# Batch 1's quantised rows transposed by DMA from SyncE's queue in place of TensorE

## The reference

```python
q1 = fake_quant(layernorm(x), x1_scale, x1_zp)      # clip(round(v / s + z), 0, 255), then (q - z) * s
q2 = fake_quant(ctx_4096, x2_scale, x2_zp)
x = x + matmul(q1, q2)                              # per batch: [1024 x 2048] @ [2048 x 2048]
y = layernorm(x)
h = einsum('td,erd->ter', y, lora_A)                # 8 experts of rank 16, two chosen by a router
x = x + y @ W_base.T + b_base + einsum('ter,eor,te->to', h, lora_B, w) * 2.0
```

## Time and profile before

| | |
|---|---|
| median of 3 runs | 991.64 us |
| profiled execution, its own time | 990.91 us |
| its span, first to last instruction | 989.2 us |
| TensorE, matmul busy | 958.8 us (97%) |
| VectorE busy | 794.6 us (80%) |
| ScalarE busy | 429.1 us (43%) |
| GpSimd busy | 146.8 us (15%) |
| TensorE's granted clock | full in every slice |
| bytes moved by DMA | 185.66 MB, 188 GB/s on average |

### The profile page before, as it was taken

How to read it: one execution, slowest core, us unless ns; L and a number is a source line. 1 busy time by engine, 2 the same in 40 slices (tenths; PEclk the granted TensorE clock), 3 DMA queues, 4 the chain that set the end, 5 groups by cost and what they waited for, 6 DMA issues and landing times.

```text
span 989.2 us, 15078 instructions
## 1 busy us (share of the span) xinstructions
PE 958.8 (97%) x5829; PEld 525.3 (53%) x5829; DVE 794.6 (80%) x1471; ACT 429.1 (43%) x466; POOL 146.8 (15%) x184
## 2 busy tenths in 40 slices
PE   2999999999999999999999999999999999999998
PEld 1766666666699444444444444444444444444444
DVE  7998988989717887997875887757889788798786
ACT  4878887755533435554443552213232323322310
POOL 3645444455100000000000000000000000000000
PEclk9999999999999999999999999999999999999999
DMA  9967676877443337867665664168533143242220
GB/s 373 371 228 297 265 275 268 295 303 267 151 139 133 108 102 227 269 213 231 228 229 171 202 232 103 57 220 287 176 109 129 69 144 118 80 151 92 87 75 33
DMA packets 62312, 185.66 MB, mean 188 GB/s; under 512 B 6896, under 2 KB 19488, under 8 KB 56096
## 3 DMA queue, kind: packets, MB, share of 16 engines
q1 hardware_dynamic: 58648, 174.18, 49.5%
q0 software_dynamic: 1280, 2.12, 2.1%
q10 hardware_dynamic: 2312, 8.39, 2.1%
HBM read 151.07 MB, written 33.60 MB: 187 GB/s over the span
## 4 chain that ended last, share of the span: by engine, by line
PE 86%; DVE 0%; issue 0%
PE pair L1877 34%; PE pair L1901 29%; PE pair L1714 13%; PE pair L1839 5%; PE pair L1849 4%; PE pair L1913 1%; PE pair L1722 0%; PE pair L1819 0%; PE pair L1693 0%; PE pair L1734 0%; DVE sq L1563 0%; DVE xt L1018 0%; DVE u L1565 0%; PE pair L1728 0%; PE pair L1813 0%; PE pair L1738 0%
## 5 line engine op out<-in xcount | busy, mean ns | idle before, releaser
L1877 PE MATMUL pair<-x2p,w_p 128*128 128x512 f16 x1536 | 337.0, 379 | 0.0
L1877 PEld LDWEIGHTS pair<-x2p,w_p 128*128 128x128 f16 x1536 | 150.3, 98 | 180.4
L1714 PE MATMUL pair<-q1T,ctx_q 128*128 128x342 f16 (+2 forms) x1584 | 228.6, 305 | 4.8 <-DVE xt L1018 2.8
L1714 PEld LDWEIGHTS pair<-q1T,ctx_q 128*128 128x128 f16 x1584 | 152.7, 97 | 75.1 <-issue 3.8
L1901 PE MATMUL pair<-x2p,w_slot 128*128 128x512 f16 x744 | 163.8, 379 | 0.0
L836 ACT ACTIVATE sq<-pair,lsc 128x512 f32<-128x512 f32 x64 | 43.5, 681 | 210.2 <-PE pair L1849 174.3
L1638 POOL TENSOR_SCALAR ctx_u<-ctx_f,par 128x512 uint8<-128x512 f32 x128 | 114.2, 905 | 109.5 <-DMA ctx_f<-in_ctx 88.4
L1901 PEld LDWEIGHTS pair<-x2p,w_slot 128*128 128x128 f16 x744 | 72.7, 98 | 87.9
L864 ACT ACTIVATE w_slot<-w_q,usc 128x1024 f16<-128x1024 f32 x32 | 36.5, 1146 | 90.8 <-DVE usc L1469 27.2
L1901 PE MATMUL pair<-x2p,x2p 128*128 128x512 f16 x336 | 74.3, 379 | 0.0
L734 ACT ACTIVATE xt<-xt,colt 128x1024 f32<-128x1024 f32 x32 | 36.7, 1146 | 55.1 <-DVE xt L1018 55.1
(11 more groups left out here) (223 smaller groups left out, 1112.8 us busy)
## 6 DMA issues: line engine op xcount, KB each, us to landing
ctx_f<-in_ctx SPq DMA_DIRECT2D x32, 1024.0 KB, 7.4
xt<-in_xT SPq DMA_DIRECT2D x32, 512.0 KB, 4.6
w_r<-in_w_n SPq DMA_DIRECT2D x32, 512.0 KB, 7.3
w_f<-in_w_t SPq DMA_DIRECT2D x32, 512.0 KB, 5.9
w_q<-in_w_t SPq DMA_DIRECT2D x32, 512.0 KB, 4.9
outT<-u SPq DMA_DIRECT2D x63, 256.0 KB, 2.7
rows<-in_x SPq DMA_DIRECT2D x15, 1024.0 KB, 9.8
x_kept<-xt ACTq DMA_DIRECT2D x16, 512.0 KB, 4.3
```

The costliest lines, as they stand in the source:

```text
L1714: ins = M.matmul(bank[at % RING][:, 0:w], ctx_q[n % NQ][:, k, :], q1T[b][:, k, t0:t0 + w], start=(k == 0), stop=(k == KT - 1))
L1877: M.matmul(base_bank(m)[:, :], w_p[j % 2][wh][:, k, :], x2p[0][:, k, xh, t], start=(k == 0 and q == 0), stop=(k == KT - 1 and q == 2))
```

## The change

For batch 1 the eight `turn` calls of TensorE are gone, 64 transposes. SyncE issues one DMA transpose per tile in their place, from the bytes of the tile (seen as 128 x 1024 16-bit pairs) into a new buffer `q1t` in SBUF (two slots). It stands behind `load_ctx` and ahead of `load_rows`, and waits for the bytes and for the copy of the tile two before. ScalarE's `ln_copy` waits for the DMA's semaphore and reads `q1t` instead of the PSUM bank; `ln_bytes_of` waits for the transfer of the tile two before. `q1t` overlaps `ar_f`, whose load moves from step 15 to step 18 and waits for all copies. `stat_sums(0)` on TensorE moves behind two chunks.

```diff
+        q1t = [place(f"q1t{s}", [P, PAIRS, P], U16, ROW_AT[1] + 2 * D * 4 + 2 * D + s * D) for s in range(2)]
...
+        q1_moved = [sem(f"q1_moved{s}") for s in range(2)]
...
+            def turn_rows(T):
+                wait_bytes(sp, T)
+                if T - TT >= 2:
+                    sp.wait_ge(q1T_copied, T - 1)
+                sp.dma_start_transpose(q1t[T % 2][:, :, :], q1u[1][T % 2][:, :].bitcast(U16)).then_inc(q1_moved[T % 2], 16)
+
...
             load_ctx(4)
             load_ctx(5)
+            turn_rows(TT)
             load_rows(TT + 2)
             for n in range(3, STEPS):
                 load_xt(n)
                 if n + 3 < STEPS:
                     load_ctx(n + 3)
+                if n == 3:
+                    turn_rows(TT + 1)
+                if n - 3 in BYTES_AT:
+                    turn_rows(BYTES_AT[n - 3])
                 if n in LOAD_AT:
                     load_rows(LOAD_AT[n])
-                if n == JT - 1:
+                if n == JT + 2:
+                    sp.wait_ge(q1T_copied, ROWS)
                     sp.dma_start(ar_f[:, :, :], ar).then_inc(ar_landed, 16)
...
-                if T % TT >= 2:
+                if b and T - TT >= 2:
+                    act.wait_ge(q1_moved[T % 2], 16 * ((T - TT) // 2))
+                elif T % TT >= 2:
                     act.wait_ge(q1_turned, T - 1)
...
-                act.wait_ge(q1_turned, T + 1)
+                if b:
+                    act.wait_ge(q1_moved[T % 2], 16 * (t // 2 + 1))
+                    turned = q1t[T % 2][:, :, :].rearrange("p m t -> p (m t)")
+                else:
+                    act.wait_ge(q1_turned, T + 1)
+                    turned = turned_bank(T)
...
-                    stat_sums(0)
                     chunk(n - 1, 2)
                     chunk(n, 2)
+                    stat_sums(0)
                     continue
                 chunk(n, 0)
-                if n == 3:
-                    turn(TT)
-                if n == 4:
-                    turn(TT + 1)
                 chunk(n, 1)
...
                 chunk(n, 2)
-                if n - 2 in BYTES_AT:
-                    T = BYTES_AT[n - 2]
-                    turn(T)
```

More of the change, by code:

```diff
@@ L7 @@
 I32 = mybir.dt.int32
+U16 = mybir.dt.uint16
 U8 = mybir.dt.uint8
@@ L717, in ln_copy @@
                 b, t = T // TT, T % TT
-                act.wait_ge(q1_turned, T + 1)
+                if b:
[4 more added lines that the diff above has]
+                    turned = turned_bank(T)
                 A.activation(q1T[b][:, :, t * P:(t + 1) * P].rearrange("p (m e) t -> p m e t", e=2),
-                             turned_bank(T).bitcast(U8).rearrange("p (m t e) -> p m e t", m=PAIRS, e=2),
+                             turned.bitcast(U8).rearrange("p (m t e) -> p m e t", m=PAIRS, e=2),
                              ACT.Identity, bias=LO1).then_inc(q1T_copied, 1)
@@ L1645, in row_bytes_of @@
                 pool.wait_ge(ln_scale, g + 1)
-                if T % TT >= 2:
+                if b == 0 and T >= 2:
                     pool.wait_ge(q1_turned, T - 1)
@@ L1686, in turn @@
                 wait_bytes(pe, T)
-                if T >= TT:
-                    pe.wait_ge(q1T_copied, T)
-                elif T >= 2:
+                if T >= 2:
                     pe.wait_ge(q1T_copied, T - 1)
```

## The result

The changed kernel takes 1003.51 us, median of 4 runs (1002.75 to 1004.29). The kernel before takes 991.64 (median of 4, 991.61 to 991.66). The ratio is 1.012, interval 1.0102 to 1.0137. So the change is **11.9 us slower**. The forecast was 997.0, 5.4 slower, in a range up to 1010: the sign and the range hold, and the measured loss is 2.2 times the forecast's. The profiled execution is the slowest of the four: 1004.29 us, its span 1002.5 against 989.2, 13.3 more.

A forecast was written before the change was run, and what follows sets the result against it. VectorE's takes were taken to set TensorE's pace up to 139 us. Late copies and rows, 2.9 + 1.1 + 1.1 + 1.0 = 6.1, less 0.9 for turns, add 5.2 us: 996.1 profiled, median 997, range 988 to 1010.

The forecast's parts named there:

- the turns are worth nothing: TensorE, batch 1: six turns before 139 us worth nothing, those of T = 14 and 15 worth 0.9 us.
- the transfer lands 0.7 us behind the context: SyncE's queue, served in order: the tile's 256 KB at 370 GB/s take 0.7 us more after the context lands.
- SyncE's own issue I take at 0.4 us, as every other one: SyncE: issuing a transpose holds it 0.4 us, making the row load behind it 1.1 us later.
- a hold of over 1 us: Sign against the forecast: SyncE held for over 1 us by a transpose.
- the late rows: Row loads behind transposes: VectorE loses 1.0 us at T = 10, 1.1 each at T = 14 and 15.
- the late copies: ScalarE's copies waiting for landings: 2.9 us in full for T = 10, 0 for the other tiles priced.
- The room of 2.5 us for T = 14: After 139 us: the take of (14,1) ends 2.5 us before (15,2) needs it, absorbing lateness.
- none later: Sign: TensorE's idle time for takes grows before (13,2) by 6 us plus the turns' 2.6, and not after.
- The forecast had 6.1 there: Before 139 us: late copies and late rows, 2.9 + 1.1 + 1.1 + 1.0 = 6.1 us.
- Hidden: Rival 1: the transfer doesn't queue behind the context and costs nothing, 990.7 us; chance 0.28, within 2 us.
- TensorE gets its 3.5 us: Rival 2: VectorE's chain keeps up, so all eight turns count, 988.1 us; chance of faster 0.12.
- The third rival's price: Rival 3, slow transposes: 2.7 us of own time each gives 1007, 7.1 us gives 1039; chance of slower still 0.15.

The follow-up runs named there:

- Without the transfer: The changed kernel with its transposes taken out, ScalarE's copies converting the bytes unturned: 991.41 us.
- The plain copy: The changed kernel with a plain SBUF to SBUF copy of the same 256 KB in place of each transpose: 998.22 us.
- transpose, row, context: The changed kernel with SyncE's context load put behind the transpose and the row load, copies where they were: 995.38 us.
- both edits and the last copy in place: The changed kernel with row loads ahead of the transposes and ScalarE's copies one step later, except that of T = 15: 994.51 us.
- copies later but the last: The changed kernel with the copies of T = 10 to 14 one step later, T = 15 and SyncE's order as in the change: 998.22 us.

## Why the prediction was right or wrong

**Right: the turns are worth nothing.** The forecast gave the 3.5 us of TensorE's work 0.9, as VectorE's takes set its pace. Without the transfer the time fell by 0.4 us (991.41 against 991.79), within what a measurement can tell.

**Right in the order, in part only in the size: the transfer lands 0.7 us behind the context.** For T = 12 it is 0.85, for T = 11 (context 104.69, copy 105.64) 0.95, for T = 13 0.83; for T = 10 and 14 it is 2.4. So for T = 10, the one copy that the forecast priced, the landing took 1.65 us more than it had. The plain copy also lands 0.6 us behind the context for some tiles (T = 11, 12, 15) and 1.6 to 2.1 for others (T = 10, 13, 14); why isn't shown. Nor do the 0.7 us hold the loads that a transpose slows (the DMA rate around T = 12, above). The whole transfer, latency and all, took 3.1 us at the soonest. The Trainium skill's 1309 ns for one 128x128 ("VectorE: DVE Perf Modes", The three transpose paths), which as an estimate would be 10.5 us for a tile's eight, is not borne out as a rate. The 350 to 400 GB/s of its "Advanced Engine Details and Errata", X-Bar Transpose, as an estimate 0.66 to 0.75 us for 256 KB, come near the 0.83 to 0.95 us of three tiles, and not the 2.4 of two.

**Wrong: "SyncE's own issue I take at 0.4 us, as every other one".** The transposes hold SyncE 1.24 to 3.05 us, and the row loads behind them 0.56 to 1.11 in place of 0.33 to 0.43. This is the term that failed; the forecast named it itself as what would make it wrong, a hold of over 1 us, and still priced it by rows of another kind of DMA. Even those weren't all 0.4: the context issued at 86.58 in the kernel before held SyncE 1.38 us. The plain copy, with a hold of 0.47 us, lands at 998.22, 1.2 above the forecast, the transpose 6.5 above; part of these 5.3 us may be the slowed loads. It can be followed for T = 14. The load went out at once after the bytes (110.28 to 110.31) and is now 2.63 us behind them (118.15 to 120.78); its landing took 7.80 us from issue to statistics and now takes 8.33. That is 3.1 us later, and VectorE's wait grew by exactly this, 1.24 to 4.37. The forecast said 1.1.

**Wrong: the late rows, 3.2 us for three tiles, each counted alone.** VectorE's waits for rows grew by 9.5 us (2.6 to 12.1): T = 10 waits 1.8, T = 13, put at 0, 2.8, and T = 14 and 15 3.1 and 1.8 more. T = 13 shows what the sum left out. Its load had no long wait behind a transpose (1.24 us), but the bytes that free its slot came late, because ScalarE had stood 4.8 us for the transpose of T = 10. The forecast added up copies and rows as if each tile began on time. They are one loop, copy, bytes, row, statistics; the run with later copies cut the rows' waits by 5.3 us.

**Wrong: the late copies, 2.9 us for T = 10 and covered elsewhere.** ScalarE waits 4.8 us for T = 10, and 3.8, 3.3 and 4.2 for T = 12, 13 and 14 (T = 13 stands in no term of the forecast); VectorE's wait for ScalarE's upper half went from 8.9 to 17.1 us. The copies' waits are worth 5.3 us in the time. The room of 2.5 us for T = 14 was real, but the 4.2 us wait used it up: TensorE waits 1.18 us at 167.11, in the part where "none later" stood.

**Not in the sum: what idling itself costs.** Seven restarts and the half clock from 114 us on are 1.1 and 2.7 us up to (13,2). With them the ledger to (13,2), the eleventh chunk before `turn_bound(1)`, closes: TensorE's idle +11.5, restarts +1.1, clock +2.7, the 48 matmuls at 98.16 +0.2, six turns -2.6, together 12.9; it starts at 151.82 where it was 139.00, 12.8 later. The forecast had 6.1 there.

**The rivals.** "Hidden" was wrong in this order of the queue; in the best one (994.51) all but 2.7 us are hidden. "TensorE gets its 3.5 us" is refuted. The third rival's price, a transfer of 2.7 us, gave 1007 and came nearer to the time than the forecast (3.5 us off in place of 6.5), by luck in good part: its 2.0 us more for each term stood for a slow landing, and what was longer was above all the issue.

What is left open: 2.7 to 3.8 us remain with the order and the copies mended. In these runs TensorE still waits 7 to 8 us for takes, 4.4 to 5 more than before, and 1.6 to 3.4 us go to the clock; against this stand the 3.5 us of turns. It isn't the same rest in both orders. With transpose, row, context VectorE's waits for rows are 4.8 us (before 2.6) and for ScalarE's upper half 10.0 (before 8.9); with both edits and the last copy in place they are 1.8 and 16.8. Whether SyncE's hold or the slowed loads are behind it wasn't told apart.

## What to carry to other kernels

Work taken off an engine that waits for another can be worth nothing, as the 3.5 us were here; look first at who sets its pace. Before a new DMA is put into a busy queue, ask four things apart: what lands ahead of it, how long its kind holds the issuing engine, what stands behind it, and whether it slows the loads beside it; if its price is known from no row of its own kind, one run of it alone is worth more than any sum. And where waits lie in a loop over several engines, a delay in one tile comes back in the next one as another wait: sum them around the loop, not tile by tile.

## What the runs showed of the hardware

- A DMA transpose of 128 x 1024 16-bit elements holds SyncE 1.24 us even with little in flight, and up to 4.6 us behind a context and a row; a plain copy of the same bytes 0.47. Eight of them add 8448 packets to the page, all of them under 512 bytes, 1056 for each 256 KB; the eight plain copies add 1153 packets, of them 129 under 512 bytes.
- Ahead of a transpose's landing behind a 1 MB load the DMA engines moved 6 to 145 GB/s for 1 to 3 us in four of the changed kernel's tiles (T = 10, 12, 13, 14), with other loads under way; with a plain copy around T = 12 381 GB/s and more.
- On ScalarE's queue beside SyncE's 1 MB loads the same transposes landed after 4.5 to 13.2 us, on SyncE's in the changed kernel after 3.2 to 9.3.
- TensorE's granted clock fell to half (0.50 from 114 to 118 us) after an idle time of 3.39 us, which cost 2.7 us. With the last copy in place it fell after 2.83 us (0.53 from 82 to 84 us; 17 chunks in 41.26 us, 1.6 more than at full clock). But with copies later but the last, 3.02 us of idle were followed by full clock (1.00 from 142 to 145 us), and after 2.0 us both are seen, by the rows of the first two fences below (0.65 from 59.5 to 64 us in the first, 1.00 from 58.8 to 63 in the second). So the length of one idle time alone doesn't decide.

TensorE's timeline, with transpose, row, context:

```profile
59.54 15.79 PE L1736 MATMUL pair<-q1T,ctx_q 128*128 128x342 f16 x96 [1.99 <-DVE ctx_q L1025]
```

and without transfer:

```profile
58.81 14.12 PE L1733 MATMUL pair<-q1T,ctx_q 128*128 128x342 f16 x96 [2.00 <-DVE ctx_q L1022]
```

and with copies later but the last:

```profile
142.15 2.48 PE L1738 MATMUL pair<-q1T,ctx_q 128*128 128x342 f16 x16 [3.02 <-DVE xt L1044]
145.27 21.14 PE L1738 MATMUL pair<-q1T,ctx_q 128*128 128x342 f16 x144 [0.64 <-DVE xt L1044]
```
